# Middle attention with split probabilities and split folded values, and a threshold search that forms its candidates ahead

## The reference, cut to what matters

```
x = x + _L1_xattn_ref(_layernorm(x), ctx, Wq, Wk, Wv, Wu, bu, qn_w, qn_b, kn_w, kn_b)
    q, k, v = heads of emb @ Wq.T, ctx @ Wk.T, ctx @ Wv.T
    q, k = _layernorm(q, qn_w, qn_b), _layernorm(k, kn_w, kn_b)
    attn = softmax(q k / 8)            # 77 keys for each of 16 heads
    return (attn @ v, heads joined) @ Wu.T + bu
```

```
scores = softmax(xt @ wg)
top_scores, sel = top_k(scores.T, CAPACITY)     # CAPACITY = 1024 of 2048 rows
```

## Time and profile before

| | us |
|---|---|
| median of 3 runs | 1705.91 (1703.36 to 1707.97) |
| the profiled execution, its own time | 1705.25 |
| its span in the trace | 1703.5 |
| PE busy in the span | 1450.4 (85%) |
| DVE busy | 1088.8 (64%) |
| ACT busy | 750.5 (44%) |
| POOL busy | 638.8 (38%) |

### The profile page before, as it was taken

One profiled execution on the slowest core, in us unless ns is written; L12 is line 12 of the kernel. 1 busy time (PEld: TensorE's weight loads), 2 busy tenths in 40 slices (PEclk: granted clock), 3 DMA queues, 4 the chain that ended last, 5 costly groups with the idle time before them and its releaser, 6 DMA issues. The chain is left out here.

```text
span 1703.5 us, 25226 instructions
## 1 busy us (share of the span) xinstructions
PE 1450.4 (85%) x9452; PEld 1209.0 (71%) x9452; DVE 1088.8 (64%) x2302; ACT 750.5 (44%) x1293; POOL 638.8 (38%) x437
## 2 busy tenths in 40 slices
PE   6997669998859999996899987669999999499774
PEld 4886558887459999995677765347888888368632
DVE  6776667975456676773464553576766665467487
ACT  2553535443137676762444342113334343145465
POOL 2461225566024455541132222022665564244100
PEclk9998979999979999997899998889999999799897
DMA  5000000000356777755000000413544443500001
GB/s 187 1 2 5 1 1 1 1 1 1 114 182 198 219 225 223 224 139 126 16 1 1 1 1 1 138 54 111 103 98 97 88 93 44 117 1 2 1 1 50
DMA packets 94175, 122.01 MB, mean 72 GB/s; under 512 B 12300, under 2 KB 79271, under 8 KB 94055
## 3 DMA queue, kind: packets, MB, share of 16 engines
q1 hardware_dynamic: 72935, 91.56, 16.7%
q0 software_dynamic: 21120, 28.85, 9.4%
HBM read 94.95 MB, written 25.43 MB: 71 GB/s over the span
## 5 line engine op out<-in xcount | busy, mean ns | idle before, releaser
L2563 POOL DMA_INDIRECT ch_total<-ch_y,ch_index x64 | 107.1, 1674 | 123.3 <-DVE ch_y L2750 108.3
L1208 POOL DMA_INDIRECT t_total<-t_y,t_index x46 | 98.1, 2132 | 133.9 <-DVE t_y L1327 108.6
L3565 POOL TENSOR_TENSOR L_s<-L_s,L_mx 128x1232 f32<-128x1232 f32 x32 | 76.5, 2389 | 125.8 <-DVE L_mx L3649 125.8
L2687 ACT ACTIVATE ch_silu<-ch_ps 128x512 f32<-128x512 f32 x64 | 38.3, 598 | 169.6 <-PE ch_ps L738 169.6
L736 PE MATMUL ch_ps<-ch_hT_hi,ch_w_hi 128*128 128x512 f32 x256 | 103.7, 405 | 10.4 <-DVE ch_hid L2776 7.0
L736 PE MATMUL t_ps<-t_hT_hi,t_w_hi 128*128 128x256 f32 x368 | 106.9, 290 | 6.0 <-DVE t_w_lo L1315 6.0
L736 PE MATMUL t_ps<-t_w_hi,t_act_hi 128*128 128x256 f32 x368 | 105.8, 288 | 0.0
L737 PE MATMUL t_ps<-t_hT_lo,t_w_hi 128*128 128x256 f32 x368 | 105.7, 287 | 0.0
L738 PE MATMUL t_ps<-t_hT_hi,t_w_lo 128*128 128x256 f32 x368 | 105.6, 287 | 0.0
L737 PE MATMUL t_ps<-t_w_lo,t_act_hi 128*128 128x256 f32 x368 | 104.1, 283 | 0.0
L738 PE MATMUL t_ps<-t_w_hi,t_act_lo 128*128 128x256 f32 x368 | 104.1, 283 | 0.0
(11 more groups left out here) (562 smaller groups left out, 4406.7 us busy)
## 6 DMA issues: line engine op xcount, KB each, us to landing
t_w_in<-in_L_ffn_w1T SPq DMA_DIRECT2D x23, 1024.0 KB, 5.3
t_w_in<-in_L_ffn_w2T SPq DMA_DIRECT2D x23, 1024.0 KB, 5.7
ch_w_in<-in_L_ffn_w SPq DMA_DIRECT2D x24, 512.0 KB, 4.0
x<-in_x SPq DMA_DIRECT2D x4, 512.0 KB, 4.9
t_total<-x SPq DMA_DIRECT2D x1, 2048.0 KB
t_rows<-t2d_h SPq DMA_DIRECT2D x1, 2048.0 KB
x<-t_total SPq DMA_DIRECT2D x8, 256.0 KB, 4.5
tb_w<-in_L_xattn_w SPq DMA_DIRECT2D x2, 1024.0 KB, 9.7
```

The costliest lines, as they stand in the source:

```text
L1208: nc.gpsimd.indirect_dma_start(out=total, out_offset=bass.IndirectOffsetOnAxis(ap=index[:, 2 * j + u:2 * j + u + 1], axis=0), in_=y[:, j % ...
L2563: nc.gpsimd.indirect_dma_start(out=total, out_offset=at(s, u), in_=y[:, s % 2, u, :], in_offset=None, compute_op=ALU.add).then_inc(added[s ...
L3565: nc.gpsimd.tensor_tensor(s[:, n % G], s[:, n % G], spread(mx[:, n % G, :], 2, [P, H, KEYS]), ALU.subtract).then_inc(shifted, 1)
```

## The change

**Attention.** The turned probabilities and the folded values are split into an fp32r high part and the rest. ACT's three copies now write `pT_hi` (the same three instructions), and DVE forms `pT_lo` from the PSUM bank and `pT_hi` (`probs_rest`, three new subtractions in each turn). PE attends by 30 products of one pass instead of ten fp32 products. PE now also waits for the subtractions: before it attends, before it uses bank 3 again for chunks 8 and 9, and before the next turn.

**Values.** ACT makes `vw_hi`: for batch 0 in the layer before (in `fp8_product`, after the jobs of group 1), for batch 1 at the start of the middle attention. DVE makes `vw_lo`: for batch 0 at the end of the layer before, for batch 1 in turns 2, 3 and 4.

**Rows.** The normalisation of the rows of tiles 8 to 15 goes from DVE's turn to the end of ACT's turn, as one Identity activation with scale and bias. Small tiles move into memory that is free by then (`w.wq`, `w.wk`, part of `vw`).

**Threshold.** The candidates of the next step are formed for all four outcomes of this one (`follow`, 4 x 4), while PE sums the counts. The choice is then made on the 16 values, and its result is the next candidates. `own` and `counts` are bf16.

```
+    def values_hi(self, b, ready):
+        for rows, fs in ((P, slice(0, FC - 1)), (LAST, slice(FC - 1, FC))):
+            self.nc.scalar.copy(self.vw_hi[0:rows, b, fs, :], self.vw[0:rows, b, fs, :]).then_inc(ready, 1)
+
+    def values_lo(self, b, lo, hi, ready):
+        for rows, fs in ((P, slice(lo, min(hi, FC - 1))), (LAST, slice(FC - 1, FC))):
+            if fs.stop > fs.start and fs.stop <= hi:
+                self.nc.vector.tensor_tensor(self.vw_lo[b][0:rows, fs, :], self.vw[0:rows, b, fs, :],
+                                             self.vw_hi[0:rows, b, fs, :].bitcast(F32), ALU.subtract).then_inc(ready, 1)
...
             def attend(n):
                 pe.wait_ge(pT_ready, 3 * n + 3)
+                pe.wait_ge(pT_lo_ready, 3 * n + 3)
+                if n == BT:
+                    pe.wait_ge(vw_lo_ready, VW_PARTS)
...
-                    ins = nc.tensor.matmul(ps[:, 7, 0:D], pT[0:rows, n % 2, f, :], vw[0:rows, b, f, :],
+                    ins = split_matmul(nc, ps[:, 7, 0:D], (pT_hi[0:rows, n % 2, f, :], pT_lo[0:rows, n % 2, f, :]),
+                                       (vw_hi[0:rows, b, f, :], vw_lo[b][0:rows, f, :]), start=(f == 0), stop=(f == FC - 1))
...
                 if n:
                     pe.wait_ge(pT_ready, 3 * n)
+                    pe.wait_ge(pT_lo_ready, 3 * n)
...
                 pe.wait_ge(pT_ready, 3 * n + 1)
+                pe.wait_ge(pT_lo_ready, 3 * n + 1)
                 turn_probs(n, 8, FC)
...
+            def normalise(t):                      # ACT, after rows_turned(n + 7) of turn n, for n + 8 < NT
+                act.wait_ge(moments_ready, 1)
+                act.wait_ge(ring_psum, place["row", t - G] + 1)
+                nc.scalar.activation(h[:, t % G, :], k.x[:, t, :], ACT.Identity, bias=shift_rows[:, t:t + 1],
+                                     scale=rstd[:, t:t + 1]).then_inc(h_later, 1)
...
+            keys.values_hi(1, vw_hi_ready)
             rows_turned(0)
...
+            def probs_rest(n, part):
+                lo, hi = 4 * part, min(4 * part + 4, FC)
+                dve.wait_ge(pT_ready, 3 * n + part + 1)
+                if n >= 2:
+                    dve.wait_ge(out_psum, n - 1)
+                nc.vector.tensor_tensor(pT_lo[:, n % 2, lo:hi, :], (the part's PSUM bank, 3 + part % 2),
+                                        pT_hi[:, n % 2, lo:hi, :].bitcast(F32), ALU.subtract).then_inc(pT_lo_ready, 1)
...
             for n in range(NT):
+                probs_rest(n, 0)
+                probs_rest(n, 1)
                 if n + AHEAD < NT:
                     take(n + AHEAD)
+                probs_rest(n, 2)
                 if n:
                     add(n - 1)
-                if n + 8 < NT:
-                    normalise(n + 8)
...
+                if n == 2:
+                    dve.wait_ge(vw_hi_ready, 2)
+                if 2 <= n < 5:
+                    keys.values_lo(1, 3 * (n - 2), 3 * (n - 1) if n < 4 else FC, vw_lo_ready)
...
+            dve.wait_ge(keys.vw_hi_ready, 2)       # fp8_product, DVE, before its last two biases
+            keys.values_lo(0, 0, FC, keys.vw_lo_ready)
...
+                if g == 1:                         # fp8_product, ACT, after the jobs of group 1
+                    act.wait_ge(keys.job_taken, keys.taken(keys.JOBS.index(("fold", 0, FC - 1))))
+                    keys.values_hi(0, keys.vw_hi_ready)
...
             for step in range(BIT_PAIRS):
-                chain(nc.vector.tensor_tensor(cand[:].bitcast(I32), thr[:].bitcast(I32).broadcast_to([P, VALUES + 1]),
-                                              pair[:], ALU.bitwise_or))
-                chain.wait()
                 for v in range(VALUES):
-                    (count of lane_probs >= cand) -> counts[:, v + 1:v + 2]
+                    (count of lane_probs >= own_cand) -> counts[:, step % 2, v + 1:v + 2]
+                if not last_step:
+                    chain(nc.vector.tensor_tensor(follow[:].bitcast(I32), spread(own_cand.bitcast(I32), 1, ways),
+                                                  spread(pair[:], 2, ways), ALU.bitwise_or))
+                    chain.wait()
                 chain(nc.vector.tensor_scalar(pair[:], pair[:], 2, None, ALU.logical_shift_right))
                 dve.wait_ge(total_ready, step + 1)
-                chain(nc.vector.scalar_tensor_tensor(out=passed[:], in0=ps_c[:, 0:VALUES + 1], scalar=float(CAPACITY),
-                                                     in1=cand[:], op0=ALU.is_ge, op1=ALU.mult))
-                chain.wait()
-                chain(nc.vector.tensor_reduce(thr[:], passed[:], AX.X, ALU.max))
+                    chain(nc.vector.scalar_tensor_tensor(out=passed[:], in0=spread(ps_c[:, 0:WAYS], 1, ways),
+                                                         scalar=float(CAPACITY), in1=follow[:], op0=ALU.is_ge, op1=ALU.mult))
+                    chain.wait()
+                    chain(nc.vector.tensor_reduce(next_cand, passed[:], AX.X, ALU.max))
```

More of the change, by code:

```diff
@@ L2385, in _ @@
             low = 1 << (2 * BIT_PAIRS - 2)
-            for v in range(VALUES + 1):
-                chain(nc.vector.memset(pair[:, v:v + 1], v * low))
-            chain(nc.vector.memset(counts[:, 0:1], float(P)))
-            chain(nc.vector.memset(thr[:], 0.0))
+            for v in range(WAYS):
+                chain(nc.vector.memset(cand[:, 0, v:v + 1].bitcast(I32), v * low))
+                chain(nc.vector.memset(pair[:, v:v + 1], v * (low >> 2)))
+            for n in range(2):
+                chain(nc.vector.memset(counts[:, n, 0:1], float(P)))
             dve.wait_ge(logits_psum, NG)
```

106 lines of the change are left out of this document (72 added, 34 removed).

## The result

| | before | changed |
|---|---|---|
| median, us | 1704.45 (1699.26 to 1707.97, 13 runs) | 1694.22 (1685.81 to 1699.23, 13 runs) |
| ratio | | 0.9938, 95% interval 0.9926 to 0.9950 |
| profiled execution, own time | 1705.25 | 1693.98 |
| its span | 1703.5 | 1692.2 |

The kernel became faster by 0.62%, some 10.6 us at the ratio. I had put 1701.5 with a range of 1694 to 1709, so the direction was right, the time lies just inside the range, 0.2 us from its fast end, and the gain was forecast at a third of its size.

The account below looks back on a forecast made before the run. Odd attention turns were taken as bound by PE, even ones by the chain to POOL's division, the search as a serial chain. Terms -8.9 + 3.9 + 1.4 + 2.6 + 1.5 - 4.2 = -3.7 gave 1701.5 us, range 1694 to 1709.

Parts of the forecast that it names:

- The likeliest case: Whole kernel: the forecast itself, -3.7 us to 1701.5, own range 1698 to 1705, chance 0.50.
- Attention product: Middle attention on PE: thirty split products take 3.77 us instead of 4.49, 0.72 back per tile where PE limits.
- Subtractions on DVE: Middle attention: three per tile, 0.69 us for 512 columns, 1.8 us a turn, not stopped by POOL.
- The case of 1721 us: Rival: POOL stops the third subtraction in each turn, even turns last 12.3, about +20 us; chance 0.10.
- Turn by turn: Middle attention, turns 0 to 10: odd turns 12.6 by PE, even ones 10.2 by DVE's lateness; sum -8.9 us.
- Low part of the values for batch 1: Three DVE pieces ending turns 2, 3, 4 make DVE late and PE wait: +3.9 us, bounds 0 and 6.
- the two prices that I weighed for a piece: Turns 2 and 4: full time after POOL's instruction, sum +3.9; or ending with it like L747, sum +2.3.
- Tail: Attention turns 11 to 15: subtractions delay `take` and the addition to x; +1.4 us, bounds 0 and +3.
- Layer before: ACT's casts ahead of a copy PE awaits: +2.6 us, PE idle 3.7; clock fall behind it 1.5 more.
- Threshold: Threshold search: bf16 saves 0.13 and the "or" 0.19 us a step, 1.95 to 1.63; -4.2, bounds -2.7 and -5.5.
- Sum: Whole kernel: -8.9 + 3.9 + 1.4 + 2.6 + 1.5 - 4.2 = -3.7 us, giving 1701.5.
- The rival that named the nearest time, 1695.7: DVE's lateness is covered: pieces +1, no clock fall, tail 0.4, threshold -4.6, sum -9.5 us; chance 0.28.

Follow-up runs that it names:

- the null: The kernel before, unchanged, timed against itself: ratio 0.9979 (0.9966 to 0.9992), 1700.73 us against 1704.43.
- the four fastest kernels: Changed kernel with row remainders before the second maximum, 1688.72; also values in idle slots, 1687.72; also low part before maximum, 1688.07; the reordering without split products, 1686.79 us.
- the attention alone: The changed kernel with the threshold search of the kernel before: 1701.49 us, ratio 0.9978 (0.9962 to 0.9994).

## Why the prediction was wrong in size

The likeliest case had the right direction and most of the mechanisms. Its sum was -3.7, the kernel gave 10.6 at the ratio. Step by step, as it put them:

- *Attention product.* Right. "Thirty of them are 3.77": 3.77 in turn 4.
- *Subtractions on DVE.* Right: the 512-wide one took 0.68, 32 of them between 256 and 440 us, none above 0.69, so POOL did not stop them. L747's successor took 2.18. The case of 1721 us did not come.
- *Turn by turn.* Odd turns to 7 12.58 for 12.6. Turn 9 stayed at 12.14, where I had 11.45, so PE's product was not its limit. Even ones 9.94 where I had 10.2: I let DVE be late in them, and it is not; PE's own work is the limit, and that I had at 10.0. Turn 10 took 9.94, not 10.9. Turns 0 to 10 without the values gave 10.5 us instead of 8.9.
- *Low part of the values for batch 1.* +1.0, +0.8 and +1.35 in turns 2, 3 and 4, 3.2 in all for 3.9; I had let a fourth turn be late. Of the two prices that I weighed for a piece the rule's was right. The piece beside POOL ended 0.8 us behind it, nearly its whole 0.94, and L747's 0.04 is no guide for it. That is the rule of the Trainium skill, page "SBUF — State Buffer", section "Who interferes with whom", that a VectorE instruction with two SBUF inputs contends with a GpSimd one that reads SBUF, and that the pair of ports which they share is an exclusive lock; the trace agrees, 0.94 against 2.66 us.
- *Tail.* Mis-sized: turns 11 to 15 cost 2.8 us for +1.4. PE waited for the addition to x 7.7 us in four turns, where it had waited 4.6 in two, and the products of turn 14 took 1.5 us more at half clock. The second has no term in the forecast and is as large as the miss.
- *Layer before.* The casts cost 2.1 us for 2.6: PE's wait was 3.24 for 3.7. The fall of the clock behind it, priced at 1.5, came in four of the six traces that have the casts, and in none of the ten without them. The layer took 3.4 to 3.8 us more with it and 2.1 without. The first trace is one of the two without it; its start-up had one stretch at 0.50 more instead (233.2 to 236.6) and took 1.6 us more. The first turned probability came 3.8, 3.4 and 2.7 us late in three traces, for 4.1. That the first of these is so near has some luck in it.
- *Threshold.* Mis-sized: 5.8 to 6.0 us in three traces for -4.2, beyond the -5.5 that I had as a bound. The pass that bf16 saves is worth 0.20 and not 0.13, the "or" 0.17 and not 0.19, so a step is 1.58 and not 1.63, 0.7 us in the twelve later steps. The two early ones took 2.16 and 2.12 and now 1.75 and 2.16, 0.4 less together where I had nothing. Both ends gave 1.0 for 0.3.
- *Sum.* This is the step that failed most: it ended at the stage's last instruction. The 2.2 us that the stage behind it gains, with 7.7 us of PE's work at 0.50 instead of 13.9, had no term. The search's term was 1.7 us too small, the turns with their tail 1.0. I had put the clock into one place, the layer before, as a price; where its other stretches fall moved as well, at a cost in turn 14 and with a gain behind the stage.

The rival that named the nearest time, 1695.7, came near by luck: it was nearer on the search (4.6), and on the clock of the layer before right in two traces of six, but not on its main step: the pieces cost 3.2, not 1, and the tail 2.8, not 0.4.

The misses in the first traces, 0.3 ahead of the turns, 1.0 in the turns with their tail, 2.2 behind, 1.7 in the search, are 5.2 together; with them the sum is -8.9. The remaining 1.7 is inside what the null showed.

What the forecast never asked was whether the split products were worth having. Its terms for them were -0.7 a turn, 11 in sixteen turns at most, and +2.6, +1.5, +3.9 and +1.4 around, so at best -1.8, and the experiments agree: the gain of the attention is the normalisation on ScalarE. What the split products save in thirteen turns, 3.1 to 4.0 us, they lose in the tail, 2.5 to 3.1, before the layer before and the values are paid. Of the loss in the tail 1.5 and 3.1 us are products at half clock.

Open is what decides where the clock falls, and so how much of a saving in PE's time is kept. I have its place in sixteen single traces, and not its cause. Also open is whether the four fastest kernels, 1686.79 to 1688.72 us, differ from each other.

## What to carry to other kernels

When two engines bound alternate turns, take the stalled instruction off the one that feeds the chain first; here this alone was worth 3.8 us in thirteen turns, and the cheaper product without it cost 10.0. Before paying for a shorter product with work on another engine, run the kernel without the product: it was equal. And look at the largest single wait ahead of a loop, 8.6 us here: its removal took an exchange of a few lines and gave 4.6 us between 190 and 531 us and 5.5 in the median, more than the change to the attention had given there (3.0 us in the changed kernel's first trace, 4.0 with the attention alone). And measure up to the end of the stage behind: it can change without an edit.

## What the runs showed that I had not expected

- The same unedited stage took 90.0 to 93.8 us, the same within 0.2 for each order of the attention ahead of it, by how long PE worked at 1.2 GHz in it (6.8 to 16.5 us).
- One stretch at 0.50 more cost 1.5 us in stages full of products, and their count changes between executions of one kernel, whose times spread from 1696.41 to 1709.41 us.
- With the rows normalised by ScalarE, the kernels with shorter products on PE had more time at half clock between 190 and 531 us: 47.8 to 58.0 us in eight traces, against 34.1 to 37.5 in three without split products. The kernel before had 47.8 to 50.1.
- PE's pause of 3.24 us in the layer before had a fall of the clock behind it in four traces and none in two; that of 2.81 in turn 12 had one.
- A two-operand instruction in SBUF took 1.56 or 3.60 us by its place beside POOL alone.
